# Graph attention kernel: the logits pass spreads and turns its values with bf16 matmuls of three parts, in place of f32 matmuls

## The reference, cut to what matters

```python
q = (h @ qw + qb).reshape(n, H, HD)          # H = 8 heads, HD = 16
k = (h @ kw + kb).reshape(n, H, HD)
v = (h @ vw + vb).reshape(n, H, HD)
logits = (q[dst] * k[src]).sum(-1) * HD ** -0.5 + (edge_attr @ ew + eb)   # edge_attr is (E, 4), ew is (4, 8)
amax = jax.ops.segment_max(logits, dst, num_segments=n)
pe = jnp.exp(logits - amax[dst])
ssum = jax.ops.segment_sum(pe, dst, num_segments=n)
w = pe / jnp.clip(ssum[dst], 1e-06)
o = jax.ops.segment_sum(w[:, :, None] * v[src], dst, num_segments=n)
```

## Time and profile before

| | us |
|---|---|
| median of three executions | 8497.92 |
| the profiled execution, its span | 11374.7 |
| convolution 1, in the profiled execution | 2944 |
| convolution 2 | 2985 |
| logits pass | 3210 |
| softmax pass | 1410 |
| all between, before and behind these | 825 |

### The profile page before, as it was taken

The page is one execution under the profiler, slowest core; times in us unless marked ns, Lnnn a source line. Parts: engine busy times, 40 slices in busy tenths (PEclk is TensorE's granted clock), DMA queues, the critical chain, the costliest instruction groups (busy, mean ns, idle before and its releaser), DMA issues. The chain is left out here.

```text
span 11374.7 us, 252728 instructions
## 1 busy us (share of the span) xinstructions
PE 8397.2 (74%) x47420; PEld 6078.2 (53%) x47421; DVE 5534.1 (49%) x14001; ACT 4454.4 (39%) x7058; POOL 4607.9 (41%) x4729
## 2 busy tenths in 40 slices
PE   2777777777737777777777567777777777799885
PEld 2444444444434444444444456666665555688775
DVE  5444444444454444445444533333344445566555
ACT  3333333333323333333333233444444445555552
POOL 1555555545515555555555144444444444100000
PEclk8778878878867778788878755555555555555555
DMA  4333333333313333333333144444444444454442
GB/s 143 92 95 94 95 94 94 93 89 94 90 31 91 90 91 94 92 94 94 91 93 91 44 130 134 135 133 132 134 131 130 125 125 123 127 161 149 140 135 85
DMA packets 986405, 1222.46 MB, mean 107 GB/s; under 512 B 302171, under 2 KB 630054, under 8 KB 984874
## 3 DMA queue, kind: packets, MB, share of 16 engines
q1 hardware_dynamic: 760558, 707.74, 21.9%
q0 software_dynamic: 225792, 514.10, 17.2%
HBM read 1079.77 MB, written 141.49 MB: 107 GB/s over the span
## 5 line engine op out<-in xcount | busy, mean ns | idle before, releaser
L794 POOL DMA_INDIRECT conv_rows<-src_table,conv_idx x3136 | 3084.6, 984 | 2780.5 <-issue 1011.3
L1213 POOL DMA_INDIRECT lg_rows<-kv_table,lg_idx x1568 | 1482.1, 945 | 1816.9 <-issue 1042.4
L714 PEld LDWEIGHTS ps<-conv_vals,conv_hot 128*128 128x128 f32 x7024 | 1136.9, 233 | 991.9 <-DVE acc L700 540.3
L897 DVE TENSOR_REDUCE conv_var<-conv_sq 128x32 f32<-128x512 f32 x784 | 536.5, 684 | 2268.4 <-ACT conv_sq L858 1930.5
L714 PE MATMUL ps<-conv_vals,conv_hot 128*128 128x129 f32 x7024 | 1196.7, 323 | 416.3 <-DVE acc L700 316.5
L858 ACT ACTIVATE conv_sq<-ps 128x512 f32<-128x512 f32 x784 | 468.1, 597 | 2521.1 <-DMA hidden<-in_x_rows 1949.4
L839 PE MATMUL ps<-conv_y,ident 128*128 128x512 f32 x1568 | 1036.5, 747 | 318.3 <-DVE conv_y L927 295.3
L634 PE MATMUL ps<-dst_parts,conv_pick 128*128 x10536 | 946.5, 239 | 427.0 <-issue 411.2
L1271 ACT ACTIVATE acc<-ps,neg_win 128x512 f32<-128x512 f32 x976 | 627.1, 684 | 1253.1 <-issue 657.4
L714 PE MATMUL ps<-sm_vals,sm_hot 128*128 128x136 f32 x3512 | 956.2, 453 | 138.1 <-DVE acc L700 78.5
L634 PE MATMUL ps<-dst_parts,lg_pick 128*128 x5268 | 653.8, 304 | 541.2 <-ACT lg_pick L619 450.3
(11 more groups left out here) (209 smaller groups left out, 11359.0 us busy)
## 6 DMA issues: line engine op xcount, KB each, us to landing
conv_dst<-dst_rows SPq DMA_DIRECT2D x784, 256.0 KB
acc<-dst_rows SPq DMA_DIRECT2D x392, 256.0 KB
v_edges<-lg_rows SPq DMA_DIRECT2D x392, 256.0 KB
sm_dst<-dst_rows SPq DMA_DIRECT2D x392, 256.0 KB, 3.3
sm_v<-v_edges SPq DMA_DIRECT2D x392, 256.0 KB, 2.6
conv_rows<-src_table,conv_idx POOLq DMA_INDIRECT x3136
conv_ea<-ea_parts SPq DMA_DIRECT2D x784, 36.0 KB
lg_rows<-kv_table,lg_idx POOLq DMA_INDIRECT x1568
```

What stands on the lines that cost most here:

```text
L714: last = pe.matmul(bank(SUMS[g])[:, 0:self.width], self.hot[g][:, j, :], vals[:, j, 0:self.width], start=(j == 0), stop=(j == TILES - 1))
L794: pool.indirect_dma_start(rows[r][:, j, :], None, src_table, bass.IndirectOffsetOnAxis(idx[r][:, j:j + 1], 0)).then_inc(S["rows_in"][r], 16)
L1213: pool.indirect_dma_start(rows[r][:, j, :], None, kv_table, bass.IndirectOffsetOnAxis(idx[r][:, j:j + 1], 0)).then_inc(S["rows_in"][r], 16)
```

## The change

In the logits pass, three things are done otherwise.

- The edge's bias. `w_ea` (f32) goes; a [39, 8] bf16 matrix `w_bias` is made once in the setup, of three parts of each weight for three parts of each attribute, and of three parts of the constant. The attributes are loaded from `ea_parts` (36 rows of bf16, which the convolutions load already). TensorE still issues four matmuls for each super, now bf16. Their bank EDGE is single instead of double, so they wait for the logits of the super before.
- The logits are turned and spread in two steps. ScalarE and VectorE split them into three bf16 parts of [128, 32] (ScalarE copies part one and two, VectorE subtracts twice). TensorE turns them with four bf16 matmuls against the identity, to 24 rows (part and head) by 512 edges in the bank TURNED; ScalarE copies these to bf16 (`by_head`); TensorE spreads them with one bf16 matmul of a constant [24, 128] matrix `head_of`, 512 columns. The widening on ScalarE (L1279) and the f32 matmuls (L1249) go. VectorE writes the logits straight into the table `logits`, and its copy (L1350) goes.
- More stages: the turn has lag 5, the spread lag 6, the maxima lag 7 (before 4 and 5). SyncE's store of v keeps lag 2 and now stands ahead of the load of the digits, which has lag 4.

In the two convolutions and the softmax pass, the matmul at the end of a super (L720) is bf16. The setup makes `head_of` and `w_bias`: one more iota, four small VectorE operations, ten for the split, two loads and twelve small DMAs within SBUF ahead of the stores of `ea_parts`.

```diff
-                pe.matmul(bank(self.spare)[:, 0:1], ident[:, :], ident[:, 0:1], start=True, stop=True).then_inc(S["vals_free"], 1)
+                pe.matmul(bank(self.spare)[:, 0:1], ident_b[:, :], ident_b[:, 0:1], start=True, stop=True).then_inc(S["vals_free"], 1)
...
-                QUERY, EDGE, AGAIN, WIDE = (0, 1), (2, 3), (4, 5), (6, 7)
-
-                PROJECT, LOGIT, WIDEN, SPREAD, TOP = 1, 2, 3, 4, 5
+                QUERY, EDGE, TURNED, AGAIN, SPREAD_TO = (0, 1), 2, 3, (4, 5), (6, 7)
+
+                PROJECT, LOGIT, STORE_V, REST, PARTS, LOAD_DIGITS, TURN, SPREAD, TOP = 1, 2, 2, 3, 4, 4, 5, 6, 7
...
                     @block.tensor
                                 pe.wait_ge(S["ea_in"][r], 16 * (k + 1))
+                                wait(pe, S["logits"], s)
                                 for j in range(TILES):
-                                    last = pe.matmul(bank(EDGE[r % 2])[:, j * HEADS:(j + 1) * HEADS], ea[r][:, j * P:(j + 1) * P], w_ea[:, :],
-                                                     start=(j == 0), stop=(j == TILES - 1), skip_group_check=True)
+                                    last = pe.matmul(edge_bias[:, j * HEADS:(j + 1) * HEADS], ea[r][:, j * P:(j + 1) * P], w_bias[:, :],
+                                                     start=True, stop=True)
                                 last.then_inc(S["query"], 1)
+                            if stage(TURN):
+                                s, r, k = stage(TURN)
+                                pe.wait_ge(S["parts"], s + 1)
+                                wait(pe, S["by_head"], s)
+                                for j in range(TILES):
+                                    last = pe.matmul(bank(TURNED)[0:3 * HEADS, j * P:(j + 1) * P], parts[r][:, j, :, :].rearrange("p k h -> p (k h)"),
+                                                     ident_b[:, :], start=True, stop=True)
+                                last.then_inc(S["turned"], 1)
...
-                                pe.wait_ge(S["wide"], s + 1)
+                                pe.wait_ge(S["by_head"], s + 1)
                                 wait(pe, S["topped"], s - 1)
-                                for j in range(TILES):
-                                    last = pe.matmul(bank(WIDE[r % 2])[:, j * P:(j + 1) * P], lg_wide[r % 2][:, j, :], ident[:, :],
-                                                     start=(j == 0), stop=(j == TILES - 1), skip_group_check=True)
-                                last.then_inc(S["spread"], 1)
+                                pe.matmul(bank(SPREAD_TO[r % 2]), head_of[:, :], by_head[r % 2][:, :], start=True, stop=True).then_inc(S["spread"], 1)
...
                     @block.scalar
-                            if stage(WIDEN):
-                                s, r, k = stage(WIDEN)
-                                act.wait_ge(S["logits"], s + 1)
-
+                            if stage(REST):
+                                s, r, k = stage(REST)
+                                act.wait_ge(S["rest"], s + 1)
+                                act.activation(parts[r][:, :, 1, :], rest[r % 2][:, :, :], ACT.Copy).then_inc(S["second_part"], 1)
+                            if stage(LOGIT):
+                                s, r, k = stage(LOGIT)
+                                wait(act, S["turned"], s - (DEPTH - 1))
+                                hold(act, S["logits"], s + 1, S["act_paced"])
+                                act.activation(parts[r][:, :, 0, :], logits_of(s), ACT.Copy).then_inc(S["first_part"], 1)
+                            if stage(TURN):
+                                s, r, k = stage(TURN)
+                                act.wait_ge(S["turned"], s + 1)
                                 wait(act, S["spread"], s - 1)
-                                act.activation(lg_wide[r % 2][:, :, :].rearrange("p j (h n) -> p (j h) n", n=WIN),
-                                               lg[r % 2][:, :].unsqueeze(2).to_broadcast([P, TILES * HEADS, WIN]), ACT.Copy).then_inc(S["wide"], 1)
+                                act.activation(by_head[r % 2][:, :], bank(TURNED)[0:3 * HEADS, :], ACT.Copy).then_inc(S["by_head"], 1)
                             if stage(0):
                                 s, r, k = stage(0)
                                 pick_act(act, S, picks, picked, span("act", s)[0], dst[r], apart, (S["dst_in"][r], 16 * (k + 1)))
...
                     @block.vector
+                            if stage(REST):
+                                s3, r3, k3 = stage(REST)
+                                dve.wait_ge(S["first_part"], s3 + 1)
+                                wait(dve, S["second_part"], s3 - 1)
+                                dve.tensor_tensor(rest[r3 % 2][:, :, :], logits_of(s3), parts[r3][:, :, 0, :], ALU.subtract).then_inc(S["rest"], 1)
+                            if stage(LOGIT):
                                 dve.wait_ge(S["dots"], s + 1)
-
-                                wait(dve, S["kept"], s - 1)
-                                wait(dve, S["wide"], s - 1)
-                                dve.scalar_tensor_tensor(lg[r % 2][:, :], dots[:, :], HD ** -0.5, bank(EDGE[r % 2])[:, 0:TILES * HEADS],
-                                                         ALU.mult, ALU.add).then_inc(S["logits"], 1)
+                                dve.scalar_tensor_tensor(logits[:, bass.ds(s, 1), :].rearrange("p a c -> p (a c)"), dots[:, :], HD ** -0.5,
+                                                         edge_bias, ALU.mult, ALU.add).then_inc(S["logits"], 1)
+                            if stage(PARTS):
+                                s4, r4, k4 = stage(PARTS)
+                                dve.wait_ge(S["second_part"], s4 + 1)
+                                dve.tensor_tensor(parts[r4][:, :, 2, :], rest[r4 % 2][:, :, :], parts[r4][:, :, 1, :], ALU.subtract).then_inc(S["parts"], 1)
...
-                            if stage(LOGIT):
-                                s, r, k = stage(LOGIT)
-                                dve.wait_ge(S["logits"], s + 1)
-                                dve.tensor_copy(logits[:, bass.ds(s, 1), :].rearrange("p a c -> p (a c)"), lg[r % 2][:, :]).then_inc(S["kept"], 1)
```

More of the change, by code:

```diff
@@ L288, in _ @@
                             sp.dma_start(w_edge[n][3 * ED * part:3 * ED * (part + 1), :], w_parts_d[n, :, :]).then_inc(w_edge_in, 16)
+                    sp.wait_ge(bias_split, 10)
+                    for part in range(3):
+                        for w_part in range(3):
+                            row = ED * (3 * part + w_part)
+                            sp.dma_start(w_bias[row:row + ED, :], bias_b[:, w_part, :]).then_inc(bias_out, 16)
+                        sp.dma_start(w_bias[9 * ED + part:9 * ED + part + 1, :], const_b[:, part, :]).then_inc(bias_out, 16)
                     sp.wait_ge(ea_cut, 3)
@@ L1199, in body @@
                                              rows[r][:, :, D:2 * D]).then_inc(S["v_out"][r], 16)
-                        slots(sp, 2, body)
+                            if stage(LOAD_DIGITS):
+                                s, r, k = stage(LOAD_DIGITS)
+                                hold(sp, S["dst_again"], s - (DEPTH - 1), S["sp_paced"])
+                                sp.dma_start(digits[r][:, :], dst_digits[:, bass.ds(s * SUPER, SUPER)]).then_inc(S["digits_in"][r], 16)
+                        slots(sp, LOAD_DIGITS, body)
                         for r in range(DEPTH):
@@ L1341, in couple @@
                                         hold(dve, S["far"], 2 * q - 1 + h, S["dve_paced"])
[L1342 removed]
+                                        dve.tensor_tensor_reduce(masked[h], bank(SPREAD_TO[r % 2]), far[h], 1.0, NEG,
                                                                  ALU.subtract, ALU.max, top[:, h:h + 1]).then_inc(S["top"], 1)
```

51 lines of the change are left out of this document (35 added, 16 removed).

## The result

The changed kernel takes 8546.5 us (median of four; 8543.9 to 8548.1) against 8498.9 us for the kernel before beside it: a ratio of 1.0054, 95% interval 1.004 to 1.0069. It is slower, where 8210 us was forecast. The first profile of before, 11374.7 us long, was taken on a chip that is slower with this kernel (see the experiments), so its stages can't be set against the profile of after.

The account below looks back on a forecast made before the run. It took GpSimd to bound the convolutions and TensorE, at the low clock, the logits and softmax passes. 8498 - 208 (logits pass) - 98 (end markers) + 17 (small losses) = 8209, say 8210 us; range 8000 to 8440.

Parts of the forecast that it names:

- the accounting of the ordinary time: Whole kernel before: 825 us outside the passes, softmax 1410, convolutions 3920 at least, leaving the logits pass 2343, 5.98 a super.
- TensorE as the bound: Logits pass before: TensorE's low-clock loop sets the pace, 6.17 us a plain super, 6.39 with further blocks.
- The halts: Convolutions and logits pass: idle stretches every second or third super, taken as a cost of being profiled.
- TensorE's new sum: Changed logits pass: TensorE's work for each super falls to 3.99 us, up to 4.4, giving back about 2 us.
- the price of four passes: Logits pass: the skill's four-pass f32 price, 1.7 us for four matmuls; by it the sum returns 1.5 us less.
- The ring through ScalarE: Changed logits pass: TensorE's pick, bias, turn, then ScalarE's copy and picks, 5.10 us plain; 5.45 taken, gaining 208 us.
- The marker, 98 us: Softmax pass: bf16 end-of-super matmul saves about 0.46 us a super, 0.25 comes through: 98 us (40 to 170).
- Setup and fill: Setup's small DMAs and VectorE operations 8 us less 2, two more slots of lag 11 us: together +17 us.
- GpSimd's floor (1): Logits pass: shorter loop or higher clock brings it to GpSimd's 5.0 us a super, gain 384 us, 8035 us; 25%.
- Transfers (2): Logits pass: gathers land late and it keeps 5.98 us a super, 8420 us; 18% together with (4).
- ScalarE as the bound (3): Logits pass: new waits make ScalarE's slot 6.5 us, the pass loses 204 us, 8620 us; 9%.
- the small bf16 matmuls cost as much as the f32 ones (4): Logits pass on TensorE: instructions, not passes, cost, so 8420 us again; 18% together with (2).

Follow-up runs that it names:

- e10: Kernel before with only the bf16 bias (w_bias, 36-row loads, EDGE still double), ordinary chip: 8478.9 us, ratio 0.9946.
- e0: Kernel before, unedited, profiled again, on a chip with halts: 11299.3 us (11277.7 beside it).
- e4: Kernel before, unedited, profiled again, on an ordinary chip without halts: 8503.8 us (8513.1 beside it).
- e14: Changed kernel, unedited, as reference on a chip with halts: 11553.0 us, ratio 1.0169 to the kernel before.
- e12: Changed kernel with ScalarE's copy of the turned bank put behind the picks, same work, chip with halts: 11491.9 us, ratio 1.0106 to the kernel before.
- e5: Changed kernel with the copy of the turned bank moved from ScalarE to VectorE, ordinary chip: 8492.0 us, ratio 0.9975 to the kernel before.
- e9: Changed kernel with half the columns of every window distance on ScalarE left out, chip with halts: ratio 1.0169 to the kernel before.
- e11: Changed kernel with half the columns of every window distance on ScalarE left out, ordinary chip: 8546.8 us, ratio 1.0022 to the kernel before.

## Why the prediction was wrong

By its own steps, in us. The measured column is the profile of after; the last column adds up to 334, the distance from 8209 (the sum that the forecast rounds to 8210) to that profile's span of 8543:

| step | forecast | measured | difference |
|---|---|---|---|
| convolutions | 3920 | 2052 + 2055 = 4107 | +187 |
| logits pass, with fill and drain | 2135 + 11 | 2200 | +54 |
| softmax pass | 1312 | 1407 | +95 |
| everything else | 831 | 829 | -2 |

- **The step that failed: the accounting of the ordinary time.** I took GpSimd's 5.0 us for the convolutions' pace, a floor, and booked all that was left over to the logits pass. Before really spends 4118 us in the convolutions (5.25 us a super) and 2153 us, 5.49 a super, in the logits pass, against my 5.98. Nearly all of the 208 us that I wanted to gain had never been there: from 5.49 to my 5.45 it is 0.04 us a super, 16 us. The sign that I named for such an error, convolutions that change by more than 1%, was no sign of it: they went from 4118 to 4107 us, 0.3%.
- **TensorE as the bound.** 6.17 us was read on a chip with halts, at the low clock. On an ordinary chip the pass has a granted clock of 0.65, and 155 of 391 slots are shorter than 4.75 us. In the first half the pace is near GpSimd's, 5.1 us a super on average in before, after and e10 alike, so what the bf16 bias takes off TensorE doesn't come back there. TensorE counts in the second half only: e10 gets 47 us out of it. The closeness of 6.39 to 5.98 that I took for support was a chance.
- **The halts.** I took them for a cost of being profiled. e0 and e4 show that they come with the chip: the profile of after has none (8543 us where I expected 10900 to 11250), and e14, on a chip with them, took 11553 us.
- **TensorE's new sum: near, 10% too high.** Forecast 3.99 us, measured 3.6 from the pick's start to the clearing's end; bias 0.19 for 0.57, turn 0.54 for 0.46, spread 0.42 for 0.53, destinations 0.40 for 0.51. The small bf16 bias was priced three times too high from the earlier trace rows. Beside it stands that the price of four passes would return 1.5 us less; by that paragraph's own terms it is 2.01 + 1.73 - 1.7, about 2.0. Nothing hangs on it.
- **The ring through ScalarE: right as a mechanism, its size nearly.** Forecast 5.10 us plain, measured 4.90; forecast 5.45 in the mean, measured 2200/392 = 5.61. It was named as what is late next. Another order alone takes 61 us off on a chip with halts (e12), and with the copy on VectorE it is 62 us of the pass on an ordinary one (e5). What I didn't see is that it takes away the short slots, from which before paid for its heavy supers. On an ordinary chip that is what the intervals suggest as the reason why the change loses and doesn't merely break even; no run there shows it by itself. A super with two couples is level in the two kernels: ScalarE's slot is 6.20 us after (6.26 before, from 6702.11 to 6708.37), with TensorE waiting 2.55 us for it now.
```profile
6699.87 1.27 ACT L1306 ACTIVATE acc<-ps,neg_win 128x512 f32<-128x512 f32 x2 [0.70 <-issue]
6701.65 1.31 ACT L1306 ACTIVATE acc<-ps,neg_win 128x512 f32<-128x512 f32 x2 [0.52 <-DVE lg_top L1391]
...
6705.54 1.53 PE L663 MATMUL ps<-dst_parts,lg_pick 128*128 x12 [2.55 <-ACT lg_pick L648]
6706.07 1.26 ACT L1306 ACTIVATE acc<-ps,neg_win 128x512 f32<-128x512 f32 x2 [0.70 <-issue]
```
- **The marker, 98 us: wrong.** The saving is half of what the weight loads promised (0.22 us), and the softmax pass isn't held by TensorE alone: a scatter waits for VectorE's addition, which takes up the rest; 3 us of the 98 came (1410 to 1407). 90% busy was no proof of a bound.
- **Setup and fill.** +10 us measured for the setup (225 against 215) where I had +6; all outside the passes grew by 8 us (821 to 829). The fill and the drain of the pipeline weren't measured apart.
- **The rivals.** GpSimd's floor (1) is nearly reached in the first half, by both kernels; the clock went down, not up. Transfers (2): the DMA share is 0.69 after and 0.75 in the faster e10, so they don't bind at that pace. ScalarE as the bound (3) had the right engine and sign, but work alone isn't it: half of the distances away moves nothing or little (e9, e11). That the small bf16 matmuls cost as much as the f32 ones (4) is refuted by the bias, 0.19 us for 1.73.

Open: how the 94 us divide between the ring, the longer pipeline, the order of SyncE's transfers and the bank EDGE, whose own wait is 12.8 us in after; the split wasn't tried. Nor is it shown on an ordinary chip that the order alone gives e5's gain back.

## What to carry to other kernels

Settle each stage's own time on a clean execution before pricing a change in one of them; a floor for one stage is not its time, and what is left over is not another's. When a step is moved so that two engines wait for each other within one slot, count not only the ring's length but the shortest slot it still allows: here the kernel whose slots can't be shorter than its ring got nothing back for its heavy supers. Look first whether another order on the waiting engine opens the ring; and take a change apart, since here one part (the bf16 bias alone, 0.9946) beat the whole.

## What was not expected of the hardware

- **Two kinds of chip.** The same kernel takes 8500 or 11300 us. Only the three passes with GpSimd's gathers differ by more than a few us: convolution 1 of after 2052 us above, and in e14
```profile
227.00:3202.00 2975.00, 2166.64 (x13092) 1321.71 (x13093) 1436.50 (x3639) 1035.99 (x1663) 1536.09 (x1568) 0.80 0.35 91
...
10025.00:11434.00 1409.00, 1197.46 (x6442) 987.74 (x6442) 845.35 (x2055) 721.39 (x1266) 0.00 (x0) 0.50 0.48 144
```
  while the softmax pass, without gathers, is 1409 against 1407 us at the same clock. VectorE's and GpSimd's busy times agree within 1% too; the time is in halts as in the earlier trace rows. Their cause isn't known, nor whether it lies in the chip or in what surrounds it; at least three chips were met with halts, one of them twice.
- **TensorE's clock fell when it had less to do, but not only then.** In the logits pass the granted clock is 0.65 with TensorE busy 95% of the time (before), 0.56 at 87% (e10) and 0.50, the lower level, at 68% (after). That agrees with the Trainium skill, "TensorE: Matmul & The Clock Gate", Part 1, by which the low clock is the default and activity releases it. The softmax pass doesn't: busy 90% before, and 0.50. Which activity counts can't be told from these rows.
